# A transformer layer in one kernel: the fill written out engine by engine, four projection banks, and integer gate weights converted on ScalarE

## The reference

```python
x = L0_attn_x                                  # (4, 512, 512)
xn = _layernorm(x, axis=-1)
# attention: qkv = xn @ w_qkv; q, k = rmsnorm(q) * q_gamma, rmsnorm(k) * k_gamma; rotary;
# causal softmax(q k^T / sqrt(32)) v; @ w_out
s = _L0_attn_ref(xn, w_qkv, w_out, q_gamma, k_gamma)
# W = (wq - 128) * scale[:, None];  down(silu(gate(xn)) * up(xn)), hidden width 1408
g = _silu(_L0_ffn_ref(xn, wq_gate, s_gate, wq_up, s_up, wq_down, s_down))
x = x + s * g
```

## Time and profile before

| | |
|---|---|
| median of three runs | 713.41 us (711.95 to 716.78) |
| profiled execution, its own time | 715.66 us |
| its span, first to last instruction | 713.6 us |
| PE busy | 658.2 us, 92% of the span |
| VectorE busy | 556.3 us, 78% |
| ScalarE busy | 445.4 us, 62% |
| GpSimd busy | 397.0 us, 56% |
| mean granted TensorE clock | 0.983 |

### The profile page before, as it was taken

How to read it: one execution, slowest core, us unless ns; L and a number is a source line. 1 busy time by engine, 2 the same in 40 slices (tenths; PEclk the granted TensorE clock), 3 DMA queues, 4 the chain that set the end, 5 groups by cost and what they waited for, 6 DMA issues and landing times.

```text
span 713.6 us, 12527 instructions
## 1 busy us (share of the span) xinstructions
PE 658.2 (92%) x3670; PEld 557.8 (78%) x3670; DVE 556.3 (78%) x1370; ACT 445.4 (62%) x988; POOL 397.0 (56%) x594
## 2 busy tenths in 40 slices
PE   3589999889999999899999998999999989979997
PEld 2578887778888788788887887887878866757886
DVE  3778888899787868997878779978786787555674
ACT  2445666677676666876766768766756676643441
POOL 5544556587666665876666658765655574510000
PEclk9789999999999999999999999999999999989999
DMA  8244443524434233134343331144452424379882
GB/s 308 86 158 150 163 163 98 168 56 119 125 99 118 92 92 103 47 113 116 108 117 100 87 108 47 53 117 144 111 173 90 145 79 119 98 210 320 277 313 104
DMA packets 62530, 94.39 MB, mean 132 GB/s; under 512 B 12032, under 2 KB 24320, under 8 KB 62336
## 3 DMA queue, kind: packets, MB, share of 16 engines
q1 hardware_dynamic: 62464, 93.59, 42.4%
HBM read 59.09 MB, written 25.82 MB: 119 GB/s over the span
## 4 chain that ended last, share of the span: by engine, by line
PE 59%; POOL 14%; DVE 8%; issue 7%; DMA 6%; ACT 3%; SPq 1%; POOLq 0%; DVEq 0%; ACTq 0%
PE bank L1215 17%; PE bank L1112 13%; PE bank L1152 6%; PE bank L1191 5%; PE bank L1241 5%; PE bank L1240 5%; POOL rr L562 4%; PE bank L1173 4%; PE bank L1124 3%; PE bank L1137 3%; POOL pp L582 3%; POOL rb L571 2%; DMA wd_raw<-w_down 2%; POOL ra L568 2%; DVE bank L926 1%
## 5 line engine op out<-in xcount | busy, mean ns | idle before, releaser
L582 POOL TENSOR_SCALAR_AFFINE_SELECT pp<-pp 128x256 fp32r<-128x256 f32 x256 | 110.9, 445 | 141.1 <-DVE pp L904 140.7
L926 DVE CUSTOM_DVE_ANT_0 bank<-bank,msk_w 128x128 f32<-128x128 f32 (+3 forms) x256 | 121.1, 508 | 44.5 <-PE bank L1173 43.7
L562 POOL TENSOR_TENSOR rr<-ss,half 128x8 f32<-128x8 f32 x64 | 109.3, 1707 | 55.4 <-DVE ss L872 55.1
L904 DVE TENSOR_TENSOR pp<-pf,pp 128x512 fp32r<-128x512 f32 (+1 forms) x192 | 131.7, 686 | 7.3 <-ACT pp L691 7.2
L1112 PE MATMUL bank<-wq,xnt_h 128*128 128x384 f32 x512 | 116.6, 351 | 13.5 <-DVE qn L884 12.0
L690 ACT ACTIVATE pf<-bank 128x512 f32<-128x512 f32 (+1 forms) x192 | 100.6, 524 | 39.2 <-PE bank L1137 30.9
L1112 PEld LDWEIGHTS bank<-wq,xnt_h 128*128 128x128 f32 x512 | 92.2, 195 | 17.8 <-issue 14.2
L1215 PE MATMUL bank<-xnt_h,wgu 128*128 128x512 f32 x352 | 98.8, 402 | 7.3 <-DVE g L954 5.4
L1152 PE MATMUL bank<-pp,va 128*65 128x512 f32 (+3 forms) x512 | 99.0, 311 | 4.7 <-POOL pp L582 4.6
L691 ACT ACTIVATE pp<-bank 128x512 fp32r<-128x512 f32 (+1 forms) x192 | 101.0, 526 | 0.0
L1215 PE MATMUL bank<-xnt_l,wgu 128*128 128x512 f32 x352 | 96.5, 396 | 0.0
(11 more groups left out here) (78 smaller groups left out, 1169.2 us busy)
## 6 DMA issues: line engine op xcount, KB each, us to landing
wgu<-wg_dram SPq DMA_DIRECT2D x66, 256.0 KB, 3.1
hf_dram<-g SPq DMA_DIRECT2D x44, 256.0 KB, 3.2
hf_raw<-hf_dram SPq DMA_DIRECT2D x16, 512.0 KB, 6.5
wg_dram<-wgu SPq DMA_DIRECT2D x22, 256.0 KB, 3.0
xr<-x SPq DMA_DIRECT2D x16, 256.0 KB, 4.5
stage<-w_gu SPq DMA_DIRECT2D x16, 256.0 KB, 3.3
oh<-oraw SPq DMA_DIRECT2D x64, 64.0 KB, 1.9
ol<-oraw SPq DMA_DIRECT2D x64, 64.0 KB, 2.0
```

Source lines behind the costliest of these rows:

```text
L562: pool.tensor_tensor(rr[:, s, :], ss[:, s, :], half[:], ALU.pow).then_inc(rr_ok, 1)
L582: op = pool.affine_select(pp[:, :, a:a + P], pp[:, :, a:a + P], [[0, 2], [1, P]], ALU.is_ge, 0.0, base=0, channel_multiplier=-1)
L904: dve.tensor_tensor(pl[:, tile], pf[:, tile], ph[:, tile].bitcast(F32), ALU.subtract).then_inc(pl_ok, 1)
L926: op = dve.tensor_tensor_reduce(bank[:, a * w:(a + 1) * w], bank[:, a * w:(a + 1) * w], msk_w[:, N - w:N], 1.0, -3.0e38, ALU.add, ALU.max, ...
```

## The change

The beats -8 to -1 go. Each engine gets a function fill() in their place, a list of calls written out by hand. The diff, cut to what the text speaks of:

```diff
-FIRST = (-3, -5, -5, -5)
-PER_BEAT = ((2, 2, 2, 2, 2, 2, 2, 2, 2, 2, 1, 1),) + ((1, 2, 2, 2, 2, 2, 2, 2, 2, 1, 1, 1, 1, 1),) * 3
+FIRST = (-2, -5, -5, -5)
+PER_BEAT = ((2,) * 11,) + ((1, 2, 2, 2, 2, 2, 2, 2, 2, 1, 1, 1, 1, 1),) * 3
+        FILL_QKV = (psum[0], psum[7], psum[5], psum[6], psum[0], psum[7])
+        FILL_XT = (psum[4], psum[2], psum[3], psum[1])
-            for c in range(-8, B * 16 + 1):
+            for c in range(B * 16 + 1):
+        LATE_W = [(g, k) for g in (G - 1, G) for k in range(KT)]
         def int_at(q):
-            a = q % 2
-            return pf[:, a * N:(a + 1) * N] if q < 6 else stage[:, (2 + a) * N:(3 + a) * N]
+            return (s_sb[:, 0, :], s_sb[:, 1, :], spare[:, 0:N])[q % 3]
...
# SyncE
+            def fill():
+                load_x(sp, 0, 0)
+                load_x(sp, 0, 1)
+                sp.dma_start(idf[:], ident).then_inc(id_in, 16)
+                load_w(0)
+                load_x(sp, 0, 2)
+                load_x(sp, 0, 3)
+                for dst, src in ((ctab, cos_tab), (stab, sin_tab), (gam[:, 0, :], q_gamma.to_broadcast([P, HD])),
+                                 (gam[:, 1, :], k_gamma.to_broadcast([P, HD]))):
+                    sp.dma_start(dst, src).then_inc(c_in, 16)
+                load_w(1)
+                for q in range(3):
+                    int_load(q)
+                sp.dma_start(msk_w[:], mask_w).then_inc(msk_in, 16)
+                load_w(2)
...
# GpSimd
+            def w_low(g, k, parts=1):
+                pool.wait_ge(w_hi, g + 1)
+                hi, lo = (wq[:, g, 0], wq[:, g, 1]) if g < G else (wo_h[:], wo_l[:])
+                pool.tensor_tensor(lo[:, k:k + parts, :].rearrange("p k n -> p (k n)"), staged(g, k, parts),
+                                   hi[:, k:k + parts, :].rearrange("p k n -> p (k n)").bitcast(F32),
+                                   ALU.subtract).then_inc(w_lp, 1)
...
+                if c < len(LATE_W):
+                    w_low(*LATE_W[c])
...
# ScalarE
+            def gu_weights(qq):
+                if qq is None or qq >= HALVES:
+                    return
+                s = qq % RING
+                act.wait_ge(wi_in[qq % 3], 16 * (qq // 3 + 1))
+                wait(act, gu_full, qq - RING + 1)
+                wait(act, wg_out[s], 16 * (qq // RING))
+                act.activation(wgu[:, s].rearrange("p k n -> p (k n)"), int_at(qq).bitcast(I32),
+                               ACT.Copy, bias=-ZERO).then_inc(wgc_ok, 1)
...
+                if c == 8:
+                    act.wait_ge(w_lp, 5 + len(LATE_W))
...
+                gu_weights(half_at(c + 1, 0))
+                gu_weights(half_at(c + 1, 1))
                 for v in SPLIT_HF.get(c, ()):
                     high(v)
...
# VectorE
+            def w_low(g, parts):
+                dve.wait_ge(w_hi, g + 1)
+                dve.tensor_tensor(wq[:, g, 1, 0:parts, :].rearrange("p k n -> p (k n)"), staged(g, 0, parts),
+                                  wq[:, g, 0, 0:parts, :].rearrange("p k n -> p (k n)").bitcast(F32),
+                                  ALU.subtract).then_inc(w_lo, 1)
...
# PE
+                    used = n if n > 5 else n - 3
+                    if n == 6:
+                        used = 5
+                    wait(pe, sq_ok, used)
+                    wait(pe, vh_ok, used)
+                    wait(pe, vl_ok, used)
+                    wait(pe, qn_ok, used)
```

More of the change, by code:

```diff
@@ L434, in beat @@
                 k = c % 4
[L435 to L440 removed]
+                if c == 1:
+                    sp.wait_ge(w_lo, 2)
+                    sp.wait_ge(w_lp, 5)
+                if c % 16 == 12 and there(c // 16 + 2, B):
+                    load_batch(c // 16 + 2)
                 first_batch(half_at(c, 0))
```

369 lines of the change are left out of this document (250 added, 119 removed).

## The result

| | before | after |
|---|---|---|
| median of 20 runs each, one chip | 713.54 us (711.95 to 717.33) | 711.16 us (705.12 to 715.90) |
| profiled execution, its own time | 715.66 us | 710.96 us |
| its span | 713.6 us | 709.2 us |
| mean granted TensorE clock | 0.983 | 0.985 |

The ratio after to before is 0.9952, with a 95% interval of 0.9938 to 0.9967: a gain of 3.4 us, a fifth of the forecast of 15.5. The medians lie 2.4 us apart; the ratio is taken over all executions but one slow one of the changed kernel (715.90 us). Of the 7.1 us that this text called the limit of a measurement it is half; with 20 runs on either side the interval still leaves out 1.

What follows compares the result with a forecast made beforehand. TensorE was taken as the bound from 60 us on, and a chain of waits through one projection bank in the fill. Terms -18.3 + 3.7 - 2.4 + 1.5 = -15.5 us took the median 713.4 to 697.9, range 692 to 706.

Steps and rivals of the forecast that it cites:

- Part 3: Two gate halves move from the fill to beats 7 and 8: +3.7 us of TensorE, 2.4 taken back from standstills.
- Part 4: GpSimd makes one low part in each of beats 0 to 7: +1.5 us, bounds 0 and 10.
- Part 1: The fill, all ahead of beat 0: first gate half at 48.2 instead of 66.49 us, a gain of 18.3 us.
- Leg A: Start of the fill, from w_qkv's landing at 12.3 us through GpSimd's roots to projection 4's low part: 25.1 us.
- Leg B: TensorE in the fill, from projection 4's last third through gate half 0 and projection 5: 6.6 us, ending at 31.7.
- rival (a): TensorE's clock stays low in the fill: 716 us, or up to 703 if it rises 10 us late; chance 0.10.
- Legs C and D: In the fill, VectorE's maxima, sums and gate: 3.7 us, to 35.4; then TensorE's gate halves 1 and 2: 5.9, to 41.3.
- Leg E: ScalarE's copies, w_out's rounding and conversions in the fill: 5.5 us, to 46.8; VectorE's 1.4 behind it, to 48.2.
- Part 2: 22 integer conversions move from VectorE to ScalarE at 0.6 us each, covered by idle time: nothing in beats 0 to 8.
- Rival (b): ScalarE's conversions become the bound: whole gain gone from 1.56 us each, 718 us at 1.8; chance 0.04.
- rival (c): GpSimd becomes the bound in beats 0 to 8: the full 10 us instead of 1.5, giving 706; chance 0.10.
- Rival (d): The fill's new banks change nothing, as GpSimd's roots and rotations, 3.2 us a unit, set the pace; no chance given.

Runs made afterwards that it cites:

- Experiment 1: Changed kernel, with unit 5's copy to tt put ahead of w_out's rounding and a conversion on ScalarE around beat 0: ratio 0.9907 to the kernel before, 709.1 us.
- Experiment 2: Changed kernel, with ScalarE's two conversions of a beat moved from ahead of tt to mid-beat: ratio 0.9920 to the kernel before, 710.2 us.
- experiment 3: Changed kernel, with ScalarE's beat 8 wait for GpSimd's last low part moved to the first write needing it: ratio 0.9906 to the kernel before, 708.4 us.
- experiment 5: Changed kernel, with the beats' integer conversions back on VectorE, the fill's left on ScalarE: ratio 1.0005 to the kernel before, 715.0 us.
- 11: The kernel of experiment 4, with GpSimd's eight low parts moved to the middle of its beat: ratio 0.9861 to the kernel before, 705.0 us.
- Experiment 14: Changed kernel, with SyncE's store and load of integers put ahead of the softmax denominators: ratio 0.9901 to the kernel before, 709.1 us.
- experiment 8: Changed kernel, with the fill's projections alternating between two banks instead of four: ratio 1.0011 to the kernel before, 715.3 us.
- experiment 4: Changed kernel, with the three ScalarE moves of Experiment 1, Experiment 2 and experiment 3 together: ratio 0.9836 to the kernel before, 703.2 us.
- Version 13: The kernel of experiment 4 with a reordered fill (w_qkv's second block early), plus SyncE's integers ahead of the denominators: ratio 0.9777 to the kernel before, 699.5 us.
- 15: Version 13, with GpSimd's eight low parts moved to the middle of its beat: ratio 0.9798 to the kernel before, 702.0 us.
- experiment 6: Kernel before, with only the change's two tables that move two gate halves out of the fill: ratio 1.0057 to the kernel before, 719.5 us.
- experiment 10: The kernel of experiment 4, with GpSimd's eight low parts of beats 0 to 7 left out: ratio 0.9856 to the kernel before, 704.5 us.
- experiment 16: The kernel of experiment 4, with SyncE's store and load of integers put ahead of the denominators: ratio 0.9810 to the kernel before, 703.0 us.

## Why the prediction was wrong

**Where the forecast was lost, by the two profiled executions.** It said 15.5 and they are 4.7 us apart. The fill was 6.0 short at the first gate half (12.3 for 18.3). A low clock behind the standstill took 1.4 more. Parts 3 and 4, forecast to cost 2.8 together, cost 4.4 between beats 1 and 9. The last 1.8 went further back, where executions of one kernel differ. So the largest step that failed is Part 1's sum, and with it the premise that behind beat 0's start "a microsecond taken off ahead of it is a microsecond off the end". Of the prediction's three signs of being wrong one came: beats 0 to 7 were longer than before, 68.0 us for 63.8. The parts in turn:

**The fill (Part 1), 18.3 forecast, 12.3 measured at the gate half.** Leg A's end, the low part that projection 4 waits for, was 27.9 instead of 25.1. Its first term failed: "I take 12.3" for the landing, which was 14.93. Behind it the leg was right: 13.0 us for my 12.8, and in the traces of 1, 2, 3, 5, 11 and 14, with landings between 13.60 and 15.73, 13.0 each time. SyncE's own issues are a third of the 2.6:

```profile
3.60 0.43 SPq L484 DMA_DIRECT2D rb<-cos_tab  x1
...
4.75 0.85 SPq L484 DMA_DIRECT2D gam<-q_gamma  x1
...
6.41 0.45 SPq L324 DMA_DIRECT2D stage<-w_qkv  x1
```

I counted bytes ahead of the block and not that the issues of the four small tables could take longer than their 0.43 us (here 0.43 to 0.85 each), which put its own issue at 6.41 instead of 5.49. The other 1.7 are the way from issue to landing, 8.5 us instead of 6.7; why it was longer stays open. The landing also scatters: with this list it was at 12.68 us in experiment 8's execution, 13.60 in 2's and 16.30 in 4's. The 768-wide subtraction, for which no row existed, was 1.85 for my 2.1. (The 1.7 that I set beside it doesn't follow from a factor of two: 740 ns for 512 is 1.1 for 768, and twice that is 2.2.) Leg B ended at 36.5 instead of 31.7, 2.0 more: its gate half took 2.9 us instead of 1.87 at a clock of 0.84, and in 13's trace, with the clock at 1.00 there, the whole leg took 7.1 us where it is 8.6 here, so the low clock is about 1.5 of the 2.0. That is a small piece of rival (a), which experiments 13 and 15 show to come and go. My reading for that rival was too strong: the kernel before was not at half speed through 20 to 40 us, its clock in the two windows was 0.71 and 0.67, a mean of both levels. Legs C and D added 0.5.

**Leg E** listed the right operations: 7.6 us from 46.6 to 54.17 for my 6.9. It failed in what it left out: I added ScalarE's queue up as if it had to be so, and did not see that TensorE had nothing else in the meantime, stood for 2.59 us and then ran 1.4 us longer at a low clock. So the lead at beat 1 was 10.9 us. Experiment 1 gives 3.2 back.

**Part 2.** The price was right: 0.63 us for my 0.6. "So nothing in beats 0 to 8" was wrong. I put the conversions against the idle time before the next exp, but they stand ahead of tt, and everything that VectorE does behind tt, the gate product last, moves with them. Experiment 2 gives 2.3 us for it by the ratios, which its trace doesn't show. Having them on ScalarE rather than on VectorE was worth 3.8 (experiment 5), more than I gave it, and the contention with Part 4's low parts is in that. Rival (b) is excluded by the price.

**Part 3.** "I take 2.4 of these 3.1 back" failed outright: nothing came back. Alone it costs 4.1 instead of 1.3 (experiment 6), an error as large as leg A's. The idle time belonged to VectorE's lateness and not to a lack of work for TensorE; a further gate half asks for a further gate product from the engine that is late.

**Part 4.** 1.5 us was right for the low parts themselves (experiment 10: 0 to 1.2), so rival (c) fell. But the wait at their end, which I named in the same sum and gave no price of its own, costs 3.3 (experiment 3; 2.0 in its trace). It stood on ScalarE ahead of tt too, long before it was needed.

**What no part had:** "The integers now have three buffers ... which can only help". They are asked for behind another thing in SyncE's list, and ScalarE, which now converts them, has the squares and the copies to tt queued behind that wait. Experiment 14 gives 3.6 alone; behind the three moves of ScalarE it is 1.9 (16 against 4). SyncE's list has this order in the kernel before too, and VectorE waited for the integers there:

```profile
130.59 0.43 DVE L965 TENSOR_SCALAR wgu<-stage 128x512 fp32r<-128x512 int32 x1 [1.45 <-DMA stage<-w_gu]
```

So mending it may gain something that was never part of the change; SyncE's new order was not tried in the kernel before.

By the ratios, taken one by one, the four bad places give 3.2, 2.3, 3.3 and 3.6, or 12.4, but the version that mends all four (16) gains 10.2 over the changed kernel; the 2.2 between are overlap, or no more than the uncertainty of the four. That makes 13.6 us to the kernel before, where I had forecast 15.5. Version 13, in which the fill has another order besides, gained 16.0. Since it isn't the kernel that I forecast, Part 3 was 2.8 too cheap in my sum and experiment 5's 3.8 were not in it, that this total agrees is luck.

**Rival (d)**, that the banks change nothing, fell by experiment 8 (4.2 us).

Left open: what of the 10.2 us the place of the conversions is, why the clock falls in one execution and not in the next, in the fill and behind beat 40, and what a version with the two gate halves back in the fill would give, which was not tried.

## What to carry to other kernels

When an operation moves to another engine, its price there is the smaller question. Look at what stands behind it in that engine's list, who waits for that, and what it waits for itself, down to the DMA's place in its own queue: here three moves of ScalarE's calls and one of SyncE's together (experiment 16) were worth three times the whole change. Idle time of the bound engine that ends in a wait for another engine is no room for more work of the kind that both must do. And when a gain at the start does not reach the end, compare the starts of the stages and find the one at which it is lost.

## What the hardware showed that I had not expected

**A short standstill of TensorE can cost a third to two thirds as much again in clock.** Between 48 and 150 us of the 18 traces there are 18 standstills of 2.01 to 2.76 us ahead of a gate half. In 17 the next eight matmuls took 2.7 to 3.55 us from their start to the next group's, 0.75 to 1.6 more than without one; the exception is the one at 133.78 above. Behind the 70 of 0.22 to 1.81 us they took 1.94 or 1.95. Over the 3 us from the gate half's start the granted clock was 0.50 to 0.67 in the 17 and 1.00 in all others, so most or all of these matmuls ran at 1.2 GHz instead of 2.4.

**Some of VectorE's operations on SBUF take longer beside GpSimd's.** The same subtraction to tt, in experiment 4, once beside GpSimd's low part and once without it:

```profile
105.78 1.54 DVE L1014 TENSOR_TENSOR tt<-qp,tt 128x256 fp32r<-128x256 f32 x1
...
117.35 0.42 DVE L1014 TENSOR_TENSOR tt<-qp,tt 128x256 fp32r<-128x256 f32 x1 [0.35 <-ACT tt L722]
...
105.75 1.28 POOL L578 TENSOR_TENSOR wo_l<-stage,wo_h 128x512 fp32r<-128x512 f32 x1
```

1.54 us against 0.42: it ends 0.3 us after GpSimd's, at 107.32. The layer norm's scaling goes from 0.54 to 1.51 us beside GpSimd's sum, and a conversion in experiment 5 from 0.41 to 1.51. Products read from PSUM stay at 0.74. The Trainium skill's GPSIMD Engine Reference, section Specifications, says that GpSimd contends with VectorE's instructions that have two SBUF inputs or run in a two-port mode; the subtraction, with two inputs in SBUF, agrees, and in which mode the other two ran no trace shows. With the conversions on ScalarE it did not decide: leaving those low parts out gained nothing (experiment 10). With them on VectorE four conversions took 1.50 us or more, in the version that lost 3.8 us (experiment 5).
